# Three banks of ten on ScalarE, VectorE adding onto its copies, GpSimd folding three sets

## What is computed

```
e = jnp.stack([tbl_0[ids[:, 0]], ..., tbl_38[ids[:, 38]]], axis=1)   # 512 x 39 x 16
x0 = xk = e
for W in [f0, f1, f2]:
    z = jnp.einsum('bfd,bgd->bfgd', x0, xk).reshape(b, f * g, d)
    xk = jnp.einsum('bpd,pm->bmd', z, W)                             # m = 128
    outs.append(xk)
z = jnp.sum(jnp.concatenate(outs, axis=1), axis=-1)
h = jnp.concatenate([z, dense_ctx], axis=1)
h = jnp.maximum(h @ W_top1 + b_top1, 0.0)
h = jnp.maximum(h @ W_top2 + b_top2, 0.0)
y = h @ W_top3
```

## Time and profile before

| | us |
|---|---|
| median of three runs | 817.92 |
| the profiled execution, its own time | 821.62 |
| its span, first to last instruction | 819.6 |
| PE busy | 738.6 |
| VectorE busy | 674.4 |
| GpSimd busy | 500.1 |
| ScalarE busy | 285.0 |
| mean granted TensorE clock | 0.981 |

### The profile page before, as it was taken

One profiled execution on the slowest core, in us unless ns is written; L12 is line 12 of the kernel. 1 busy time (PEld: TensorE's weight loads), 2 busy tenths in 40 slices (PEclk: granted clock), 3 DMA queues, 4 the chain that ended last, 5 costly groups with the idle time before them and its releaser, 6 DMA issues.

```text
span 819.6 us, 11557 instructions
## 1 busy us (share of the span) xinstructions
PE 738.6 (90%) x3366; PEld 581.9 (71%) x3366; DVE 674.4 (82%) x2209; ACT 285.0 (35%) x786; POOL 500.1 (61%) x515
## 2 busy tenths in 40 slices
PE   0987999989999999989999999988998999999977
PEld 0975777767677877767677876767777876767657
DVE  4853989988997589988997589987998579999960
ACT  2313333334342234433442233433343243334311
POOL 6886888765785467765785467744464345555330
PEclk9997999999999999999999999999999999999989
DMA  9730000000000000000000000000000000000000
GB/s 225 166 119 3 3 4 4 3 3 3 2 4 2 2 2 4 3 1 4 3 2 3 2 4 2 3 1 0 2 1 1 0 1 1 0 2 1 1 1 1
DMA packets 13101, 12.06 MB, mean 15 GB/s; under 512 B 3952, under 2 KB 11856, under 8 KB 12785
## 3 DMA queue, kind: packets, MB, share of 16 engines
q1 hardware_dynamic: 8494, 10.15, 4.6%
q0 software_dynamic: 4544, 1.17, 1.4%
HBM read 11.31 MB, written 0.00 MB: 14 GB/s over the span
## 4 chain that ended last, share of the span: by engine, by line
PE 39%; DVE 34%; POOL 16%; issue 9%; ACT 2%; DMA 0%; POOLq 0%; ACTq 0%; DVEq 0%
DVE acc L568 23%; POOL emb L305 8%; PE y L689 8%; PE y L691 7%; PE y L690 7%; PE side L707 5%; POOL z_parts L315 4%; DVE z L534 4%; PE acc L671 2%; DVE diag L576 2%; POOL sum L330 2%; DVE acc L565 2%; PE side L718 2%; PE rep L659 1%; DVE x_lo L540 1%
## 5 line engine op out<-in xcount | busy, mean ns | idle before, releaser
L568 DVE SCALAR_TENSOR_TENSOR acc<-y,x_rows,acc 128x128 f32<-128x128 f32 x1856 | 503.3, 340 | 75.6 <-PE y L691 74.9
L689 PE MATMUL y<-w_hi,x_hi 128*128 128x512 f32 (+1 forms) x640 | 273.1, 427 | 2.1 <-DVE x_lo L540 1.6
L691 PE MATMUL y<-w_hi,x_lo 128*128 128x512 f32 (+1 forms) x640 | 250.0, 391 | 0.0
L690 PE MATMUL y<-w_lo,x_hi 128*128 128x512 f32 (+1 forms) x640 | 249.5, 390 | 0.0
L416 ACT ACTIVATE scaled<-y,x_rows 128x128 f32<-128x128 f32 x512 | 145.8, 368 | 243.8 <-PE y L691 237.3
L315 POOL TENSOR_TENSOR z_parts<-z,z_parts 128x512 fp32r<-128x512 f32 x112 | 144.1, 1288 | 54.2 <-ACT z_parts L378 53.9
L305 POOL DMA_INDIRECT emb<-in_tbl_dram,ids_sb x142 | 152.1, 1071 | 32.8 <-issue 20.2
L689 PEld LDWEIGHTS y<-w_hi,x_hi 128*128 128x128 f32 x640 | 121.4, 190 | 35.7 <-DVE acc L568 8.1
L321 POOL TENSOR_TENSOR sum<-scaled 128x512 f32<-128x512 f32 x64 | 82.5, 1290 | 92.8 <-ACT scaled L416 90.9
L691 PEld LDWEIGHTS y<-w_hi,x_lo 128*128 128x128 f32 x640 | 121.0, 189 | 25.5
L690 PEld LDWEIGHTS y<-w_lo,x_hi 128*128 128x128 f32 x640 | 121.6, 190 | 24.5
(11 more groups left out here) (68 smaller groups left out, 557.2 us busy)
## 6 DMA issues: line engine op xcount, KB each, us to landing
w_sb<-in_w_dram SPq DMA_DIRECT2D x1, 2496.0 KB, 9.9
emb<-in_tbl_dram,ids_sb POOLq DMA_INDIRECT x142
s_sb<-in_w_dram SPq DMA_DIRECT2D x12, 160.0 KB
w_sb<-in_small_tables_dram SPq DMA_DIRECT2D x1, 980.0 KB
wt_sb<-in_ids_small_dram SPq DMA_DIRECT2D x1, 896.0 KB
wt_sb<-in_W_top_dram SPq DMA_DIRECT2D x1, 768.0 KB
s_sb<-in_w_dram SPq DMA_DIRECT2D x4, 144.0 KB
scaled<-in_selectors_dram SPq DMA_DIRECT2D x1, 532.0 KB
```

The lines of the kernel that those rows point to most:

```text
L568: dve.scalar_tensor_tensor(part, term, x0_f, part, ALU.mult, ALU.add).then_inc(terms_in, 1)
L689: pe.matmul(dst, x1_hi[:, t % 2, cols], hi, start=True, stop=False)
L690: pe.matmul(dst, x1_hi[:, t % 2, cols], lo, start=False, stop=False)
L691: pe.matmul(dst, x1_lo[:, t % 2, cols], hi, start=False, stop=True).then_inc(y_ready, 1)
```

## The change

`BY_ACT` becomes (0, 3, 6): ScalarE empties three banks of each block, and the other seven are VectorE's. `acc` goes. VectorE adds each of its 27 terms in place onto the scaled copies of the ScalarE bank before it: banks 1 and 2 onto those of bank 0, banks 4 and 5 onto those of bank 3, banks 7, 8 and 9 onto those of bank 6, field i of a bank onto copy i. So the first VectorE bank behind each ScalarE bank waits for that bank's copies, and a later term waits for the term four before. GpSimd's `fold_two`, called at j = 7, adds the first two sets once VectorE is through bank 5; `finish_x2`, still at j = 0 of the next block, adds the third set (512 wide), folds to 256 and to 128. The file is three lines shorter, so its line numbers shift.

```diff
-BY_ACT = (1, 5)
+BY_ACT = (0, 3, 6)
+FOLD_AT = 7
...
-        acc = sb("acc", [P, 2, 2, M])
...
-            def fold_scaled(k):
-
-                pool.wait_ge(y_act, act_banks(BANKS * k + BANKS - 1))
+            def fold_two(k):
+
+                pool.wait_ge(terms_in, dve_terms(BANKS * k + BY_ACT[2] - 1))
                 pool.tensor_tensor(sum4[:, :], scaled[:, k % 2, 0, :], scaled[:, k % 2, 1, :],
                                    ALU.add).then_inc(four_in, 1)
-                pool.wait_ge(four_in, k + 1)
+
+            def finish_x2(k):
+
+                pool.wait_ge(terms_in, dve_terms(BANKS * k + BANKS - 1))
+                pool.wait_ge(four_in, 2 * k + 1)
+                pool.tensor_tensor(sum4[:, :], sum4[:, :], scaled[:, k % 2, 2, :], ALU.add).then_inc(four_in, 1)
+                pool.wait_ge(four_in, 2 * k + 2)
                 pool.tensor_tensor(sum2[:, :], sum4[:, 0:2 * M], sum4[:, 2 * M:4 * M], ALU.add).then_inc(two_in, 1)
-
-            def finish_x2(k):
-
-                pool.wait_ge(terms_in, dve_terms(BANKS * k + BANKS - 1))
-                pool.wait_ge(two_in, 2 * k + 1)
-                pool.tensor_tensor(sum2[:, :], sum2[:, :], acc[:, k % 2, :, :].rearrange("p a m -> p (a m)"),
-                                   ALU.add).then_inc(two_in, 1)
                 if k >= 2:
                     pool.wait_ge(s_ready, k - 1)
-                pool.wait_ge(two_in, 2 * k + 2)
+                pool.wait_ge(two_in, k + 1)
                 pool.tensor_tensor(x2_sb[:, k % 2, :], sum2[:, 0:M], sum2[:, M:2 * M], ALU.add).then_inc(x2_in, 1)
...
-                    if j == BY_ACT[-1] + 1:
-                        fold_scaled(k)
+                    if j == FOLD_AT:
+                        fold_two(k)
...
                 if j == BY_ACT[0] and k >= 2:
-                    act.wait_ge(four_in, k - 1)
+                    act.wait_ge(four_in, 2 * (k - 1))
...
-                if j == 0 and k >= 2:
-                    dve.wait_ge(x2_in, k - 1)
                 first = dve_terms(n) - len(fields_of(j))
-                in_block = first - dve_terms(BANKS * k) + len(fields_of(0))
+                h = sum(1 for a in BY_ACT if a < j) - 1
+                if j == BY_ACT[h] + 1:
+                    dve.wait_ge(y_act, act_banks(n - 1))
                 for i, f in enumerate(fields_of(j)):
                     x0_f = x0_rows[:, t // TPG % 2, k % (TPG * NBLK), f:f + 1]
-                    part = acc[:, k % 2, (in_block + i) % 2, :]
-                    term = y2[n % RING][:, i * M:(i + 1) * M]
-                    if in_block + i < 2:
-                        dve.tensor_scalar(part, term, x0_f, None, ALU.mult).then_inc(terms_in, 1)
-                    else:
-                        dve.wait_ge(terms_in, first + i - 1)
-                        dve.scalar_tensor_tensor(part, term, x0_f, part, ALU.mult, ALU.add).then_inc(terms_in, 1)
+                    part = scaled[:, k % 2, h, i * M:(i + 1) * M]
+                    if j > BY_ACT[h] + 1:
+                        dve.wait_ge(terms_in, first + i - FPB + 1)
+                    dve.scalar_tensor_tensor(part, y2[n % RING][:, i * M:(i + 1) * M], x0_f, part,
+                                             ALU.mult, ALU.add).then_inc(terms_in, 1)
```

More of the change, by code:

```diff
@@ L316, in low_part @@
                                    ALU.subtract).then_inc(z_lo_in, 1)
-            def fold_scaled(k):
-                pool.wait_ge(y_act, act_banks(BANKS * k + BANKS - 1))
+            def fold_two(k):
+                pool.wait_ge(terms_in, dve_terms(BANKS * k + BY_ACT[2] - 1))
                 pool.tensor_tensor(sum4[:, :], scaled[:, k % 2, 0, :], scaled[:, k % 2, 1, :],
                                    ALU.add).then_inc(four_in, 1)
-                pool.wait_ge(four_in, k + 1)
-                pool.tensor_tensor(sum2[:, :], sum4[:, 0:2 * M], sum4[:, 2 * M:4 * M], ALU.add).then_inc(two_in, 1)
             def finish_x2(k):
                 pool.wait_ge(terms_in, dve_terms(BANKS * k + BANKS - 1))
-                pool.wait_ge(two_in, 2 * k + 1)
-                pool.tensor_tensor(sum2[:, :], sum2[:, :], acc[:, k % 2, :, :].rearrange("p a m -> p (a m)"),
-                                   ALU.add).then_inc(two_in, 1)
+                pool.wait_ge(four_in, 2 * k + 1)
+                pool.tensor_tensor(sum4[:, :], sum4[:, :], scaled[:, k % 2, 2, :], ALU.add).then_inc(four_in, 1)
+                pool.wait_ge(four_in, 2 * k + 2)
+                pool.tensor_tensor(sum2[:, :], sum4[:, 0:2 * M], sum4[:, 2 * M:4 * M], ALU.add).then_inc(two_in, 1)
                 if k >= 2:
                     pool.wait_ge(s_ready, k - 1)
-                pool.wait_ge(two_in, 2 * k + 2)
+                pool.wait_ge(two_in, k + 1)
                 pool.tensor_tensor(x2_sb[:, k % 2, :], sum2[:, 0:M], sum2[:, M:2 * M], ALU.add).then_inc(x2_in, 1)
```

## The result

The changed kernel takes 835.8 us (median of four runs, 835.4 to 836.8), against 818.1 for the kernel before in the same comparison: 1.0204 times as long, 95% interval 1.0173 to 1.0234. The profiled execution's span went from 819.6 to 833.7 us, 14.1 more. The forecast was 830, in a range of 808 to 845, and 12 more on the span.

A forecast was written before the change was run, and what follows sets the result against it. VectorE was taken to bound ordinary tiles, TensorE part of layer 3 tiles. Ordinary tiles +15, tiles 0 and 1 +5, layer 3 +4, columns -9, last tile -2.7 made +12 us: forecast 830, range 808 to 845.

The forecast's parts named there:

- `x1_low` to P4: From slot 36 to VectorE's product at the next slot 4: slot 36's bank becomes ScalarE's, -0.83 us.
- P4 to P8: Between VectorE's products at slots 4 and 8: new stall at slot 7 for ScalarE's copies, +0.78 us.
- P8 to P24: Between VectorE's products at slots 8 and 24: GpSimd's longer block end delays TensorE at slot 14, +0.73 us.
- P24 to P28: Between VectorE's products at slots 24 and 28: new stall at slot 27 for ScalarE's copies, +0.78 us.
- P28 to `x1_low`: From VectorE's product at slot 28 to slot 36: GpSimd's longer block end delays TensorE's bank 35, +0.68 us.
- The stalls for copies: VectorE waits for ScalarE's copies queued behind the high part: 0.78 us at slots 7, 27; 1.04 at 11, 31.
- The longer block end: GpSimd's finish_x2 takes 2.69 us before the low part, which starts 1.39 us later and delays TensorE's contract.
- 1 (nothing stalls): Whole kernel: ScalarE's waiting hides its added copies, ordinary tiles fall to TensorE's 36 us, 774 us; chance 0.05.
- Rival 2: Slots 10 and 30: GpSimd's longer block end doesn't reach VectorE, 801 to 803 us; chance 0.13.
- third and fifth term: Ordinary tile's delays from GpSimd's longer block end, behind slots 8 and 28: +0.73 and +0.68 us.
- Rival 3: Whole kernel: half of the GpSimd delay bites and the effects cancel, 818 +- 7 us; chance 0.22.
- Rival 4: Gathering tiles: GpSimd falls behind for good, 2.5 us a tile over ten tiles, 855 us; chance 0.06.

The follow-up runs named there:

- e1: Changed kernel with GpSimd making the low part first at slots 10 and 30, finish_x2 behind it: 808.7 us, ratio 0.988.
- e6: Changed kernel without the 512-wide fold of the third set in finish_x2 (set missing from x2), end in its old place: 805.3 us, ratio 0.9797.
- e9: Changed kernel with the third set's fold left out of x2 and ScalarE's high part one slot later: 777.4 us, ratio 0.949.
- e10: Changed kernel with low part first, high part one slot later and the block's end 256 + 256 + 128 wide: 789.3 us, ratio 0.9628.
- e3: Changed kernel with ScalarE's high part one slot later (HIGH_LAG 3 for 2): 824.5 us, ratio 1.0068.
- e7: Changed kernel with the same sum reordered on GpSimd, the block's end folding 256, 256 and 128 wide: 822.9 us, ratio 1.0023.
- e5: Kernel before the change with one more 512-wide GpSimd add on spare data ahead of finish_x2's folds: 868.9 us, ratio 1.0599.
- e4: Changed kernel with the low part ahead of finish_x2 and ScalarE's high part one slot later: 796.5 us, ratio 0.9722.

## Why the prediction was right, point by point

Along tile 7 (39.5 before; after by the forecast's steps; after measured), and tile 13 of four experiments:

| stretch | before | forecast | after | e1 | e6 | e9 | e10 |
|---|---|---|---|---|---|---|---|
| `x1_low` to P4 | 8.91 | 8.08 | 8.26 | 8.07 | 7.97 | 7.97 | 8.09 |
| P4 to P8 | 3.70 | 4.48 | 4.55 | 4.56 | 4.56 | 3.70 | 3.71 |
| P8 to P24 | 16.05 | 16.78 | 16.84 | 15.66 | 15.69 | 15.48 | 14.84 |
| P24 to P28 | 3.70 | 4.48 | 4.55 | 4.56 | 4.56 | 4.05 | 4.04 |
| P28 to `x1_low` | 7.15 | 7.83 | 7.79 | 6.63 | 6.63 | 6.45 | 6.17 |
| tile | 39.5 | 41.65 | 42.0 | 39.5 | 39.4 | 37.7 | 36.9 |

The sum was right, 12 forecast and 14.1 measured on the span, and so was the mechanism, stretch by stretch. That it came out this near is in part luck: the ordinary tiles grew by 2.2 us more than forecast and the last tile shrank by 1.8 less, and the layer 3 tiles took back 2.1.

- *VectorE loses four terms a block.* Its work fell by 55 us, not by the 66 that I gave as a sign. 256 terms fewer at 0.258 are 66; the busy time counts overlaps once, and with every stall a chain of terms ends and its last one counts with its full 0.34. There are some 85 more such stalls (156 against 71), 7 us, and diag takes some 3 more (estimates). A term itself is 341 ns, 340 before, with its wait four back: that step held.
- *The stalls for copies.* Forecast 0.78 and 1.04; the rows show 0.76 or 0.77 and 1.02 or 1.03, counted from the recorded end of the last term, 0.08 behind the pitch by which I had counted, so that they are 0.06 to 0.07 longer than forecast. The handover from ScalarE to VectorE takes 0.10 us (405.78 to 405.88), not the 0.03 that I took from the other direction; the stretches P4 to P8 and P24 to P28 are each 4.55 and not 4.48. That the stalls come from the high part ahead of the bank is shown by e3 and e9, where P4 to P8 is back at 3.70; P24 to P28 comes down to 4.05 only, where VectorE waits 0.26 us at slot 27 for a bank of PE's (in e9 its last matmul ends at 668.38, and VectorE starts at 668.42).
- *The longer block end.* Forecast 2.69, measured 2.67, and both stretches behind it within 0.06 of the forecast. That it is the low part's start that costs is shown three ways: e1 moves it, e6 and e7 shorten the end, e5 adds the cost to the kernel before. The rule of the Trainium skill, GPSIMD Engine Reference, § Engine selection, against elementwise adds on GpSimd pointed the right way; the runs add that the duration hurts through what stands behind it in the queue, since e1 keeps the add there and is faster than before.
- *`x1_low` to P4* was 0.18 too small. Two causes are in the trace: the bank of slot 37 starts 0.89 and not 0.81 behind `x1_low`, and diag takes 0.82 of VectorE's time and not 0.74, lasting 0.89 us beside POOL's fold where it lasted 0.81.
- *The sum by tiles.* Ordinary tiles +17.2 (forecast +15); tiles 0 and 1 +4.7 (+5); layer 3 tiles +1.9 (+4); column tiles -8.9 (-9); the last tile -0.9 (-2.7); 14.0 of the span's 14.1. The layer 3 tiles and the last were missed by the clock, which no step of mine had. Up to the start of tile 15 the kernel before has falls in tiles 0, 8 and 10 (58.2 and 51.3 in the last two, against 56.6 and 49.5), the changed kernel in tiles 1, 10 and at the start of 15. Layer 3 tiles without one grew by 1.2, my 1.4, and the last, without its fall, would have gained about 2.4, my 2.7 (an estimate: the bank of slot 37 starts 2.40 behind `x1_low` there, 0.89 in tile 7). Three falls stand on either side, so they shift the parts and hardly the sum, which is luck too.
- *Tiles 0 and 1*: I spread 2.5 on each; it was 0.9 and 3.8. The parts are nearer than they look. Of the 3.8, about 1.5 is a fall of the clock in tile 1 that the kernel before has not, and the 0.9 is short by about 1.0 for the fall in its tile 0 that the changed kernel has not (`x1_low` to P4 of tile 0 is 6.97 without such a fall, after the change, and 8.00 with one, in e4). At equal clock that makes 1.9 and 2.3 (estimates).
- *The rivals.* 1 (nothing stalls) and 2 (the block end doesn't reach VectorE) fell by the 1.95 us at slot 34 and VectorE's 1.07 us for the bank of slot 35. Rival 2's arithmetic for a kernel without the third and fifth term, an ordinary tile of 38.5 and 801 to 803 us, is what e1 and e6 made: 39.4 to 39.5, 809 and 805. Its price was right to a microsecond a tile; only its condition failed. Rival 3 (it cancels, 818) fell by the time. Rival 4 (POOL behind for good in tiles 0 to 9) did not come about in the changed kernel, whose tiles 3 to 9, with gathers, take the same 42.0 as 11 to 14 without; in e10 gathers do cost, 39.4 to 39.9 against 36.9. The rule that moving work off a saturated VectorE to Scalar may pay (the Trainium skill, Perfetto Trace Analysis, § Optimizing Scalar/DVE Operations) was right of the work and not of this placing of it: 836 as changed, 789 with three pieces moved.

## What to carry to other kernels

With in-order queues, a busy share says what an engine could give, not what a change brings: work out, for each wait that a change adds, what stands ahead of the awaited instruction in its queue, and for each instruction made longer, what stands behind it. Before you put a difference between two kernels down to one stall, compare stretches at the same granted clock and look for instructions that the move has brought together: the same move read as 11 and as 28 us here, and was 0.9 and 1.7 us a tile at full clock, 0.56 of that difference from one instruction beside another. A poor first result (11 us here) is then no reason to give up an idea. And order a helper engine's queue by who waits: here one call moved behind another was worth 27 us, with the same work.
